# Two attention-and-experts layers of a four-layer kernel, ordered by batch, with one division per 512 queries

## The reference, cut to what matters

```
h = layernorm(x);  n = rms(h)
q, k, v = n @ wq', n @ wk', n @ wv'          # 16 heads of 8 features
q, k = rms(q) * qn_w, rms(k) * kn_w          # per head
a = softmax(causal(q @ k' / sqrt(8))) @ v    # per head, 1024 x 1024
h = h + a @ wo'                              # from feature 32 on
n = rms(h)
w = the two largest of softmax(n @ gate_w'), scaled to sum 1
y = w0*E0(n) + w1*E1(n) + w2*E2(n) + w3*E3(n)
x = x + h + y
```

## Time and profile before

| | value |
|---|---|
| median of three runs | 1206.76 us |
| profiled execution, its time / its span | 1207.07 / 1205.2 us |
| busy: PE, PEld | 674.5 us (56%), 333.1 us (28%) |
| busy: DVE | 867.5 us (72%) |
| busy: ACT | 506.5 us (42%) |
| busy: POOL | 403.4 us (33%) |
| first F layer | about 468 to 783 us |
| second F layer | about 886 us to the end |
| exponentials L1445, x320 | 268.1 us busy |
| reciprocals L1554, x32 | 107.3 us busy |
| chain that ended last | DVE 47%, PE 23%, ACT 16%, issue 10% |

### The profile page before, as it was taken

The page is one execution under the profiler, slowest core; times in us unless marked ns, Lnnn a source line. Parts: engine busy times, 40 slices in busy tenths (PEclk is TensorE's granted clock), DMA queues, the critical chain, the costliest instruction groups (busy, mean ns, idle before and its releaser), DMA issues.

```text
span 1205.2 us, 11485 instructions
## 1 busy us (share of the span) xinstructions
PE 674.5 (56%) x4014; PEld 333.1 (28%) x4014; DVE 867.5 (72%) x1306; ACT 506.5 (42%) x752; POOL 403.4 (33%) x334
## 2 busy tenths in 40 slices
PE   4990000040004004479899799963264799978997
PEld 2450000040004003222222556631243122225655
DVE  6899999999999995856657733269959557667212
ACT  3423000122220001579999322243034899973321
POOL 1250847600006602226765000006802566650000
PEclk9985555555555556779999799987565899997999
DMA  2250006172000020223310000000003242100001
GB/s 92 70 140 1 1 0 140 35 168 63 13 14 14 0 35 0 84 75 116 97 33 22 1 1 1 1 0 1 0 0 115 63 142 54 54 1 1 1 1 35
DMA packets 30258, 50.71 MB, mean 42 GB/s; under 512 B 4472, under 2 KB 14328, under 8 KB 29176
## 3 DMA queue, kind: packets, MB, share of 16 engines
q1 hardware_dynamic: 29432, 49.32, 15.2%
q10 hardware_dynamic: 768, 0.66, 0.3%
HBM read 20.98 MB, written 16.92 MB: 31 GB/s over the span
## 4 chain that ended last, share of the span: by engine, by line
DVE 47%; PE 23%; ACT 16%; issue 10%; POOL 1%; DMA 1%; ACTq 1%; POOLq 0%; SPq 0%; DVEq 0%
ACT PX L1445 10%; PE PS L1330 6%; PE PS L1308 5%; PE PS L1350 4%; PE PS L1289 3%; DVE D L813 2%; DVE S L817 2%; DVE P L814 2%; DVE PS L871 2%; DVE PRD L870 2%; DVE mag L1031 2%; DVE PA L772 2%; ACT P L688 2%; DVE RO L837 2%; DVE RP L832 2%
## 5 line engine op out<-in xcount | busy, mean ns | idle before, releaser
L1445 ACT ACTIVATE PX<-PS 128x1024 f32<-128x1024 f32 (+1 forms) x320 | 268.1, 1016 | 12.1 <-PE PS L1271 12.1
L1224 POOL TENSOR_TENSOR PX<-PX,maskf 128x256 f32<-128x256 f32 (+1 forms) x192 | 173.4, 931 | 125.0 <-ACT PX L1445 124.5
L1289 PE MATMUL PS<-PX,VA 128*32 128x512 f32 (+3 forms) x1536 | 166.2, 503 | 22.3 <-POOL PX L1224 14.5
L1617 DVE SCALAR_TENSOR_TENSOR X<-PS,wts,X 128x96 f32<-128x96 f32 x128 | 38.4, 315 | 118.2 <-PE PS L1350 103.9
L1271 PE MATMUL PS<-QS,KS 64*128 64x512 bf16 (+3 forms) x768 | 107.8, 339 | 16.7 <-issue 11.4
L1554 DVE RECIPROCAL DEN<-DEN 128x512 f32<-128x512 f32 x32 | 107.3, 3353 | 1.1
L580 PE MATMUL PS<-ones,HT 64*128 64x1 f32 x64 | 13.0, 348 | 152.0 <-ACT HT L672 152.0
L947 POOL TENSOR_TENSOR PRQ<-PA,LQK 128x2048 f32<-128x2048 f32 (+15 forms) x16 | 39.9, 2520 | 151.8 <-DMA WS<-S 138.6
L1552 DVE LOAD_MASK_SELECT DEN<-PS x32 | 0.4, 14 | 107.2 <-PE PS L1289 93.5
L591 PE MATMUL PS<-awout,V 64*128 64x128 f32 x64 | 13.3, 422 | 110.5 <-DVE vss L820 110.5
L1308 PE MATMUL PS<-HT,fw 128*128 128x512 f32 x144 | 71.2, 638 | 3.9 <-DVE HG L1584 2.6
(11 more groups left out here) (264 smaller groups left out, 1649.5 us busy)
## 6 DMA issues: line engine op xcount, KB each, us to landing
QS<-qs_d SPq DMA_DIRECT2D x32, 196.0 KB
qs_d<-QP SPq DMA_DIRECT2D x24, 256.0 KB, 3.9
ks_d<-QP SPq DMA_DIRECT2D x24, 256.0 KB, 4.0
KS<-ks_d SPq DMA_DIRECT2D x32, 192.0 KB
K<-LQK SPq DMA_DIRECT2D x16, 256.0 KB
W<-WS SPq DMA_DIRECT2D x16, 256.0 KB, 4.1
qkv_d<-CY SPq DMA_DIRECT2D x3, 1024.0 KB, 3.9
LQK<-qkv_d SPq DMA_DIRECT2D x8, 256.0 KB, 4.9
```

Of the source, the lines that this page charges most:

```text
L1224: pool.tensor_tensor(block, block, bcast(maskf[:], 1, 2 * halves), ALU.mult).then_inc(probs_masked, 1)
L1289: last = pe.matmul(PS[32 * h:32 * h + 32, SCORES_BANKS + qc, c0:CH], VA[b][:, kt, h, :], px[:, i % 2, at:at + CH - c0], start=(kt == 0), s ...
L1445: act.activation(tile(PX[u % PDEPTH][:]), tile(PS[:, k:k + 2, :]), ACT.Exp).then_inc(probs_ready, 1)
```

## The change

It reorders the F layers by batch.

- Preparation: batch 0 is transposed, projected and prepared first, batch 1's projections follow. Batch 1's squares, high, middle and third parts, shifts, their root and its transposes stand between attention's units (`beside(u)` in the streams of TensorE and ScalarE, calls between `heads_out` in VectorE's). SP stores batch 1's parts between the loads of groups 2 and 3.
- Batch 0's output projection, join, second norm and router stand inside batch 1's attention (units 94 to 126 of 160), batch 1's inside batch 0's experts.
- Scores have two pairs of banks (`DEPTH` = 2); banks 4 and 5 (`SIDE_BANKS`) are for the work beside.
- The denominators of four groups are gathered in `DEN` by the same kind of multiply that gathers the sums, and one shuffle, one reciprocal and one product follow for each 512 queries: 4 times a layer.
- The experts run for one batch and then the other, with two pairs of banks for hidden layers.
- `XL` is made right after `SQ`, and the output is stored in two halves.

```diff
-        DEPTH = 3
+        DEPTH = 2
         OBANKS = 2
-        SCORES_BANKS = 2 * DEPTH
-        ROUTER_BANK = 5
-        HT_BANKS = 4
-        F_RES = NCH + TILES + 2 * NCH + NCH + NCH + 1
-
+        SIDE_BANKS = 4
+        O_BANKS = 6
...
+            stores(0)
+            sp.wait_ge(parts_stored, PARTS * (rep * B + 1))
+            for it in range(3):
+                stack(it)
+            stores(1)
+            stack(3)
+            sp.wait_ge(parts_stored, PARTS * (rep * B + 2))
+            for it in range(4, B * NG):
+                stack(it)
...
+            turned(0, 0, 0)
+            project(0, (2, 3, 4, 5, 6, 7, 0, 1), (0, 0, 0, 0, 0, 0, 0, 0))
+            pe.wait_ge(qkv_read, rep * TILES + 2)
+            turned(1, 0, 2)
+            project(1, (4, 5, 6, 7, 0, 1, 2, 3), (3, 4, 5, 6, 7, 8, 0, 0))
+            pe.wait_ge(qk_normed, rep * B + 1)
+            pe.wait_ge(qkv_read, rep * TILES + TB + 4)
+            for c in range(CB):
+                qk_turned(c, 4 + 2 * c)
+            pe.wait_ge(qkv_read, rep * TILES + TB + 6)
+            shifts_turned(0, 0)
+            pe.wait_ge(qkv_read, (rep + 1) * TILES)
+            pe.wait_ge(m_read, rep * NCH + CB)
+
+            def beside(u):
+                if u == 10:
+                    pe.wait_ge(qk_normed, rep * B + 2)
+                    qk_turned(CB, SIDE_BANKS)
+                elif u == 16:
+                    pe.wait_ge(rest_ready, 2 * (rep * NCH + CB + 1))
+                    qk_turned(CB + 1, SIDE_BANKS)
+                elif u == 24:
+                    pe.wait_ge(rest_ready, 2 * (rep * NCH + CB + 2))
+                    shifts_turned(1, SIDE_BANKS)
+                elif u == HALF + 14:
+                    out_project(0)
+                elif u == HALF + 28:
+                    turned(0, 1, SIDE_BANKS)
+                elif u == HALF + 38:
+                    router(0)
...
+            for b in range(B):
+                c0, c1 = b * CB, b * CB + 1
+                read = rep * STEPS + b * 14
+                gated = rep * NCH + b * CB
+                if b:
+                    pe.wait_ge(ht_read, 2 * (rep + 1) * NCH)
+                    pe.wait_ge(up_read, read - 1)
+                up(c0, 0, F_E1A)
+                pe.wait_ge(up_read, read)
+                up(c0, 2, F_E1B)
+                pe.wait_ge(up_read, read + 1)
+                up(c1, 0, F_E1A)
+                if b == 0:
+                    pe.wait_ge(router_read, rep * B + 1)
+                    out_project(1)
+                    pe.wait_ge(o_read, OBANKS + (rep + 1) * B * NG * 2)
+                down1(b, 0)
+                pe.wait_ge(h1_ready, gated + 1)
+                up(c1, 2, F_E1B)
+                pe.wait_ge(up_read, read + 2)
+                up(c0, 0, F_E2)
+                down1(b, 1)
+                pe.wait_ge(h1_ready, gated + 2)
+                up(c0, 2, F_E0)
+                pe.wait_ge(up_read, read + 3)
+                up(c0, 0, F_E3, 1)
+                pe.wait_ge(up_read, read + 4)
+                mid(2, 0, [HA[:, k, :] for k in range(2)])
+                pe.wait_ge(up_read, read + 5)
+                mid(0, 4, [HE[:]])
+                pe.wait_ge(up_read, read + 6)
+                mid(2, 2, [HB[:, k, :] for k in range(2)])
+                pe.wait_ge(up_read, read + 7)
+                up(c1, 0, F_E2)
+                pe.wait_ge(up_read, read + 8)
+                up(c1, 2, F_E0)
+                down(b, 0)
+                pe.wait_ge(up_read, read + 9)
+                up(c1, 0, F_E3, 1)
+                pe.wait_ge(up_read, read + 10)
+                mid(2, 0, [HA[:, k, :] for k in range(2)])
+                pe.wait_ge(up_read, read + 11)
+                mid(0, 4, [HE[:]])
+                pe.wait_ge(up_read, read + 12)
+                mid(2, 2, [HB[:, k, :] for k in range(2)])
+                if b == 0:
+                    turned(1, 1, SIDE_BANKS)
+                pe.wait_ge(up_read, read + 14)
+                down(b, 1)
+                if b == 0:
+                    router(1)
...
+            act_sqrt(act, ask, stat[:])
+            act_sqrt(act, ask, stat[:])
+            turned(0, 0)
+            project(0, (2, 3, 4, 5, 6, 7, 0, 1))
+            act_sqrt(act, ask, qst[:, 0:TB])
+            turned(CB, 2)
+            project(1, (4, 5, 6, 7, 0, 1, 2, 3))
             q_squares(0)
-            high(0)
+            high(0, 4)
             q_root(0)
-            high(1)
+            high(1, 6)
+            mid(0)
+            shifts(0, 0)
+            mid(1)
             act_sqrt(act, ask, qst[:, TB:2 * TB])
-            shifts(0)
-            shifts(1)
-            mid(0)
-            mid(1)
-            q_squares(1)
-            high(2)
-            q_root(1)
-            high(3)
-            shifts(2)
-            shifts(3)
-            mid(2)
-            mid(3)
+
+            def beside(u):
+                if u == 8:
+                    q_squares(1)
+                elif u == 12:
+                    high(CB, SIDE_BANKS)
+                elif u == 15:
+                    q_root(1)
+                elif u == 18:
+                    high(CB + 1, SIDE_BANKS)
+                elif u == 21:
+                    mid(CB)
+                elif u == 25:
+                    mid(CB + 1)
+                elif u == 28:
+                    shifts(1, SIDE_BANKS)
+                elif u == HALF + 22:
+                    act_sqrt(act, ask, stat[:, 0:TB])
+                elif u == HALF + 32:
+                    turned(NCH, SIDE_BANKS)
+                elif u == HALF + 46:
+                    router(0)
...
-                    v.stream_shuffle(DEN[:], o, [HD * (g + 1) % 32] * 32).then_inc(den_ready, 1)
-                    v.wait_ge(den_ready, 2 * at + 1)
-                    v.reciprocal(DEN[:], DEN[:]).then_inc(den_ready, 1)
-                    v.wait_ge(den_ready, 2 * at + 2)
-                    v.scalar_tensor_tensor(out=DEN[:] if g else AO[:, t:t + CH], in0=o, scalar=frows[:, g:g + 1],
-                                           in1=DEN[:], op0=ALU.mult, op1=ALU.mult).then_inc(o_read, 1)
-                    if g:
-                        v.wait_ge(o_read, OBANKS + at + 1)
-                        v.tensor_tensor(AO[:, t:t + CH], AO[:, t:t + CH], DEN[:], ALU.add).then_inc(heads_added, 1)
-                        added += 1
-            first = base + NCH + TILES + 3 * NCH
...
+                if g == 0:
+                    v.tensor_scalar(AO[:, t:t + CH], o, mine, None, ALU.mult)
+                    v.tensor_scalar(DEN[:, t:t + CH], o, after, None, ALU.mult).then_inc(o_read, 1)
+                else:
+                    v.scalar_tensor_tensor(out=AO[:, t:t + CH], in0=o, scalar=mine, in1=AO[:, t:t + CH],
+                                           op0=ALU.mult, op1=ALU.add)
+                    v.scalar_tensor_tensor(out=DEN[:, t:t + CH], in0=o, scalar=after, in1=DEN[:, t:t + CH],
+                                           op0=ALU.mult, op1=ALU.add).then_inc(o_read, 1)
+                if g == NG - 1:
+                    v.wait_ge(o_read, OBANKS + at + 1)
+                    link(v.stream_shuffle(DINV[:], DEN[:, t:t + CH], [(r + HD) % 32 for r in range(32)]))
+                    link(v.reciprocal(DINV[:], DINV[:]))
+                    v.tensor_tensor(AO[:, t:t + CH], AO[:, t:t + CH], DINV[:], ALU.mult).then_inc(ao_ready, 1)
+
+            def heads_added(b):
...
+            q_k_squares(0)
+            q_k_normed(0)
+            q_k_rest(0, 4)
+            q_shifts(0)
+            q_k_rest(1, 6)
+            q_k_squares(1)
+            q_k_normed(1)
+            heads_out(0, 0)
+            q_k_rest(CB, SIDE_BANKS)
+            q_shifts(1)
+            q_k_rest(CB + 1, SIDE_BANKS)
+            heads_out(0, 1)
+            q_k_third(CB)
+            q_k_third(CB + 1)
+            for it in range(1, NG):
+                heads_out(it, 0)
+                heads_out(it, 1)
+            heads_out(NG, 0)
+            heads_added(0)
+            second_squares(0)
+            heads_out(NG, 1)
+            second_normed(0)
+            heads_out(NG + 1, 0)
+            heads_out(NG + 1, 1)
+            logits(0)
+            heads_out(NG + 2, 0)
+            weights(0)
+            heads_out(NG + 2, 1)
+            heads_out(NG + 3, 0)
+            heads_out(NG + 3, 1)
...
+            gate(0, 0)
+            heads_added(1)
+            gate(0, 1)
+            second_squares(1)
+            v.wait_ge(x_sum, rep * B + 1)
+            add1(0, 0)
+            add1(0, 1)
+            second_normed(1)
+            add_rest(0, 0)
+            add_rest(0, 1)
+            v.wait_ge(down_read, (rep * B + 1) * DOWNS)
+            v.nop().then_inc(x_half, 1)
+            logits(1)
+            gate(1, 0)
+            gate(1, 1)
+            weights(1)
+            v.wait_ge(x_sum, rep * B + 2)
+            add1(1, 0)
+            add1(1, 1)
+            add_rest(1, 0)
+            add_rest(1, 1)
...
```

(39 more changed lines are left out.)

477 lines of the change are left out of this document (227 added, 250 removed).

## The result

The changed kernel takes 1215.22 us in the median of 15 runs (1210.5 to 1219.71), the kernel before 1205.2 beside it (1203.33 to 1212.34): ratio 1.0071 [1.0052, 1.009]. The forecast was 1212, within 1%. The profiled execution took 1210.5 us, the lowest of the 15; part of the difference is therefore not in the profile, and I come back to it. Medians in this document leave out three single runs far above all others: 2692.3 and 1285.16 us of the kernel before, 3631.68 us of the one with the join behind attention.

The account below looks back on a forecast made before the run. ScalarE's exponentials bound attention, TensorE close behind; TensorE bounds the stage after it. Attention +46.4, first scores -10.2, behind attention -29.5 and output -1.8 give +4.9 on 1207.07: 1212 us, range 1199 to 1227.

Parts of the forecast that it names:

- 1. First scores: Before attention: batch 0's head sums start sooner and its remainder waits less, so first scores come 5.1 us earlier per layer.
- 2 to 4. Attention: Attention: moved ScalarE work +13.4, moved TensorE work +4.1, two score-bank pairs +6.7, overlap -1.0; +23.2 us per layer.
- two pairs: Attention's score banks: two pairs instead of three make ScalarE idle more, +6.7 us per layer, bounds 0 and 10.
- parts 2 and 3: Work moved into attention: ScalarE's work and four table switches +13.4 us, TensorE's uncovered blocks +4.1 us per layer.
- the 1.0 taken off for overlap: Attention: nine ScalarE blocks fill idle gaps already counted for two score-bank pairs, 0.1 us each, -1.0.
- Rival C: ScalarE in attention: table switches cost twice their row, 8 more times 1.28, +10.2 us, total 1222; chance 0.04.
- Rival B: Attention: TensorE becomes the bound through two score-bank pairs and its blocks, +22.7 us, total 1230; chance 0.17.
- D: Attention: a block comes before its input and ScalarE stands, half a group lost per layer, +10, 1222 us; chance 0.08.
- A: Attention: two score-bank pairs suffice and TensorE's blocks vanish under ScalarE's, -18.7 us, total 1188; chance 0.13 including towards it.
- 5: VectorE's division within attention: one per 512 queries, 24 of 32 reciprocals go, 80 us of VectorE, gain 0.
- 6: Stage behind attention: 103.9 us instead of 118.4 and 118.9, so -14.5 and -15.0; bounds 102 and 109.
- 7: Output transfer at the end: stored in halves, the first under batch 1's experts, -1.8 us, once.

Follow-up runs that it names:

- the join behind: Changed kernel with batch 1's preparation ahead of attention, three pairs of score banks throughout, batch 0's join, norm and router after attention: 1202.16 us, ratio 0.9952.
- the stand filled: Changed kernel with preparation ahead, three score-bank pairs until unit 83, then two, plus 20 unread transposes where TensorE idled: 1189.04 us, ratio 0.9845.
- three then two, again: Changed kernel with batch 1's preparation ahead and three score-bank pairs until unit 83, two after it; repeat run: 1191.27 us, ratio 0.9869.
- both kernels without the root: Copy replaces batch 0's second-norm root: in the changed kernel 1210.89 us; with preparation ahead and three score-bank pairs until unit 83, then two, 1185.87 us.

## Why the prediction was right, and where it was not

The total was right, at 1212 against 1210.5 in the profiled execution; the median is another 5 us up, inside the range. The change itself was forecast at +4.9 us: the two profiled executions differ by 3.4, the medians by 10.0. So the time that no profile shows (6.6) is larger than the forecast change, and that the median lies within 0.3% of the forecast is partly luck. By its steps, per layer:

*1. First scores.* −5.7 and −5.0 measured, −5.1 forecast, closer than the 2 us by which single profiles differ here. (The lower bound of 2.6 was added up wrongly: 2.6 and 1.0 without the projection give 3.6.) The kernel with all of batch 1's preparation ahead of attention starts its scores just as early, and it keeps the new order of batch 0 ahead of its stores, which therefore carries the gain. What was moved on ScalarE and TensorE had been hidden by stores and loads anyway, so its price in attention was pure loss.

*2 to 4. Attention.* Forecast +23.2, measured +22.3 and +22.9. The parts, split in the first layer by the place of the unit, changed kernel against the one before with two pairs (starts of exponentials; the preparation stands in units 8 to 28, the join in 94 to 126). Subtracting whole stages instead would give 11.3 for the join and 5.9 for the preparation, since the kernel between them, with preparation ahead, has TensorE at its lower clock for longer:

| us per layer | priced | measured | from |
|---|---|---|---|
| two pairs | 6.7 | 5.2 | 146.40 − 141.22 |
| batch 0's join inside | about 8 | 9.3 | units 80 to 159: 79.63 − 70.31 |
| batch 1's preparation inside | about 9 | 7.8 | units 0 to 79: 80.02 − 72.20 |

The priced column sorts the terms of parts 2 and 3 by batch: the join has two changes, root, copies, exponential (4.2) and TensorE's blocks (4.0); the preparation has 6.4 of ScalarE's work and two changes (2.7). With the 1.0 taken off for overlap the priced parts make 23.1. So the total came out in part by errors that cancel. Three terms were mis-sized:
- *Preparation, too dear by 1.3.* ScalarE is busy 16.30 of 17 us where two pairs run alone (560 to 577), so its blocks have 0.7 of idle time to fill there; the 0.1 a block that I took off covers part of it.
- *The join, too cheap by 1.1.* TensorE's clock stands in no term of the sum. With the stand filled and the clock at 1.00, units 80 to 159 take 78.46 us, 8.2 above two pairs alone, which is the price. Where the clock fell they take 79.63 (changed kernel), 80.98 (three then two, again) and 81.46 (preparation ahead). So the clock cost 1.2 to 3.0 us a layer, 1.2 of it in the changed kernel; this compares kernels that differ in score banks ahead of unit 84. Without the root the join still costs 6.9 in the changed kernel (77.25 − 70.31), where the prices leave 5.3: values that wait for POOL's mask take part of what ScalarE saves.
- *Two pairs.* 0.66 in a later group instead of 0.84, for the reason given with the experiment.

Rival C is excluded by both kernels without the root. The medians give 1.5 (6.1 / 4) and 1.4 (5.4 / 4) a switch, the group of the root in the trace 1.2, near the load's row of 1.28. The Trainium skill, "ScalarE: Activation LUTs" (What ACT_TABLE_LOAD costs), has 2.66 us a switch; these runs do not agree with it. Rival B's TensorE bound does not hold in steady attention; in the 4 us behind the stand TensorE is the bound, by its clock. D did not happen: the wait ahead of the root's table load is 0. A's idea that blocks fit in fails on the join's 9.3, and its idea that two banks suffice on the 5.2.

*5.* 0, shown. *6.* Forecast 103.9, measured 103.72 and 102.77, and here too errors cancel. TensorE idles only 2.9 and 2.3 us, where I listed 4.8 of waits: the last HC 1.11 for 1.4, silu 0.67 and 0 for 0.9, H0 twice 0.26 for twice 0.45, the last division 0.2 for 0.4, and none above 0.15 for the join of batch 1. TensorE's own work is 100.8 in the first layer instead of 99.1. *7.* −1.9 against −1.8.

*Not predicted.* The B layer between the F layers is 1.8 us longer, though its code is the same. Its first spectral matmuls run at the lower clock for longer: the first twelve take 5.36 us before and 7.10 after. The same two windows before and after (columns as in the earlier trace rows; the layer begins 1.7 us later in the second pair):

```profile
793.00:798.00 5.00, 4.23 (x16) 2.43 (x15) 3.02 (x4) 2.28 (x4) 0.00 (x0) 0.78 0.00 0
798.00:803.00 5.00, 3.84 (x10) 1.16 (x9) 1.11 (x1) 3.08 (x3) 0.00 (x0) 1.00 0.00 0
```

```profile
793.00:798.00 5.00, 3.99 (x17) 3.19 (x17) 4.53 (x10) 2.39 (x4) 0.00 (x0) 0.50 0.00 0
798.00:803.00 5.00, 5.00 (x8) 1.53 (x9) 0.00 (x0) 0.00 (x0) 0.00 (x0) 0.65 0.00 0
```

*Open.* Of the medians' 10.0 us the profiled executions show 3.4. The profile of the kernel before stands 1.9 above its median, and the changed kernel's (1210.5, 1211.12) are at the low end of its runs, the first 4.7 below the median. In its 15 runs the time goes with TensorE's mean granted clock: the eight at 0.773 or more have a median of 1213.2 us, the seven at 0.770 or less 1217.9. That points to more stretches at the lower clock in those runs; where they lie, no trace shows. Some kernels spread less (three pairs then two, 1190.66 to 1192.57) and some as much (the stand filled, 1184.89 to 1192.22; the join behind, 1197.57 to 1207.22), all with preparation ahead, so its place does not decide it.

## What to carry to other kernels

Work that already lies under a transfer is free where it is; moved beside an engine that bounds a stage, it costs most of its length (here 7.8 of 9 us). When a block is put into a tight pipeline, price also the stand that it forces on the next engine and the clock that this engine comes back at; useless work in the stand can be cheaper than the stand. Where a buffer is given up for such a block, give it up only for the units in which the block needs it.

## What the runs showed of the hardware

TensorE's granted clock fell to 0.72 in the stretch behind a stand of 3.25 us inside a stage that held 1.00 ahead of it, and stayed at 1.00 once 2.4 us of the stand were filled. How long it stays low behind the same stand differs between kernels: over units 100 to 119 the mean was 0.93 in the changed kernel and 0.83 with preparation ahead, and the group took 1.65 us longer. The same twelve spectral matmuls of the B layer, behind the same code, took 5.36 us in one kernel and 7.89 in the next; the sixteen transposes ahead of them took 4.02 in both:

```profile
785.07 4.02 PE L447 MATMUL PS<-ident,XL 128*128 128x128 f32 x16 [4.36 <-DVE XL L432]
789.78 5.36 PE L985 MATMUL PS<-HT,bwf 128*65 128x512 f32 x12 [0.69 <-ACT HT L455]
```

```profile
782.44 4.02 PE L447 MATMUL PS<-ident,XL 128*128 128x128 f32 x16 [4.36 <-DVE XL L432]
787.14 7.89 PE L985 MATMUL PS<-HT,bwf 128*65 128x512 f32 x12 [0.69 <-ACT HT L455]
```

Of the thirteen B layers measured here, seven took 106.7 to 107.6 us and six 109.0 to 109.4, and no edit touches this layer. What decides between the two is not known from these runs. A difference of 2 us between two of these kernels can be nothing but this.
